# An attention and mixture-of-experts layer: routing work of VectorE gathered into fewer slots, and two PSUM readers moved behind the transposes

## The reference

```
xn  = layernorm(x)
att = attention(rmsnorm(xn) * norm_scale)      # 16 heads of 64, softmax over 512 keys, output projection + bias
lg  = silu(xn @ rw1 + rb1) @ rw2 + rb2         # router: 128 -> 512 -> 8 experts
top 2 of the 8 logits, softmax over the two    # the weights of a token
ffn = sum over its 2 experts of weight * (silu(xn @ w1[e] + b1[e]) @ w2[e] + b2[e])
out = x + att + ffn
```

## Time and profile before

| | |
|---|---|
| median of 3 runs | 2036.31 us (2034.46 to 2036.4) |
| profiled execution | 2034.46 us |
| its span, first to last instruction | 2032.5 us |
| TensorE busy | 1862.8 us, 92% |
| VectorE busy | 1629.2 us, 80% |
| ScalarE busy | 1238.5 us, 61% |
| GpSimd busy | 706.7 us, 35% |
| chain that ended last | TensorE 29%, VectorE 29%, ScalarE 27%, issue 13% |
| mean granted clock of TensorE | 0.994 |

### The profile page before, as it was taken

One profiled execution on the slowest core, in us unless ns is written; L12 is line 12 of the kernel. 1 busy time (PEld: TensorE's weight loads), 2 busy tenths in 40 slices (PEclk: granted clock), 3 DMA queues, 4 the chain that ended last, 5 costly groups with the idle time before them and its releaser, 6 DMA issues.

```text
span 2032.5 us, 72807 instructions
## 1 busy us (share of the span) xinstructions
PE 1862.8 (92%) x31718; PEld 1106.8 (54%) x31718; DVE 1629.2 (80%) x2274; ACT 1238.5 (61%) x3009; POOL 706.7 (35%) x624
## 2 busy tenths in 40 slices
PE   8898888889988888989899999999999999999996
PEld 5554455555545555555455555555555555555554
DVE  6887888888888888888988787878787777777774
ACT  5555556555665566556566666666757575757562
POOL 3243543344444333433102423333324132423142
PEclk9999999999999999999999999999999999999999
DMA  3033221111111111111323333433334334333342
GB/s 95 15 77 101 75 88 51 35 44 44 45 34 44 42 32 28 44 39 39 86 78 76 71 80 66 85 67 78 72 73 73 77 67 84 69 77 70 70 70 48
DMA packets 148863, 127.48 MB, mean 63 GB/s; under 512 B 27040, under 2 KB 133408, under 8 KB 148512
## 3 DMA queue, kind: packets, MB, share of 16 engines
q1 hardware_dynamic: 117952, 102.10, 18.8%
q0 software_dynamic: 30592, 20.73, 7.6%
HBM read 90.59 MB, written 34.27 MB: 61 GB/s over the span
## 4 chain that ended last, share of the span: by engine, by line
PE 29%; DVE 29%; ACT 27%; issue 13%; DMA 2%; SPq 0%; POOL 0%; POOLq 0%; DVEq 0%; ACTq 0%
ACT PR L907 19%; DVE NM L568 12%; DVE PT L576 7%; PE pair L469 7%; PE pair L330 6%; PE pair L311 6%; DVE OT L585 3%; ACT ZZ L996 3%; PE pair L343 2%; ACT ZT L993 2%; PE pair L272 2%; DVE HH L811 1%; PE pair L296 1%; PE pair L240 1%; PE pair L223 1%
## 5 line engine op out<-in xcount | busy, mean ns | idle before, releaser
L907 ACT ACTIVATE PR<-pair,NM 128x512 f32<-128x512 f32 x1024 | 690.5, 686 | 566.3 <-DVE NM L568 566.1
L576 DVE STREAM_TRANSPOSE PT<-PR 128x1024 f32<-128x1024 f32 x512 | 630.1, 1239 | 90.4 <-ACT PR L907 72.7
L568 DVE TENSOR_REDUCE NM<-pair 128x2 f32<-128x1024 f32 x512 | 599.8, 1212 | 52.6 <-PE pair L311 52.2
L311 PE MATMUL pair<-KS,QS 64*32 64x512 f32 x8192 | 505.7, 597 | 13.1 <-ACT KS L883 6.7
L330 PE MATMUL pair<-PT,V 32*64 32x256 f32 x16384 | 482.0, 378 | 15.8 <-issue 7.1
L1157 POOL DMA_INDIRECT out<-YS,IDW x156 | 245.1, 1571 | 657.8 <-DVE YS L818 612.1
L330 PEld LDWEIGHTS pair<-PT,V 32*64 32x64 f32 x16384 | 380.0, 131 | 167.6 <-issue 118.4
L311 PEld LDWEIGHTS pair<-KS,QS 64*32 64x32 f32 x8192 | 126.1, 106 | 242.4 <-issue 174.0
L811 DVE SCALAR_TENSOR_TENSOR HH<-ZT,ZZ 128x512 f32<-128x512 f32 x156 | 104.9, 692 | 171.6 <-ACT ZT L993 95.7
L1106 POOL TENSOR_TENSOR TH<-TH,HS 128x512 f32<-128x512 f32 x64 | 81.8, 1277 | 376.2 <-ACT HS L947 376.2
L907 ACT ACTIVATION_READ_ACCUMULATOR PR<-pair,NM 128x1 f32 x1024 | 208.0, 203 | 0.0
(11 more groups left out here) (130 smaller groups left out, 1743.1 us busy)
## 6 DMA issues: line engine op xcount, KB each, us to landing
RB<-l_rows SPq DMA_DIRECT2D x128, 256.0 KB
E<-w_tab SPq DMA_DIRECT2D x39, 512.0 KB
XG<-slots SPq DMA_DIRECT2D x39, 264.0 KB, 4.2
E<-in_w SPq DMA_DIRECT2D x39, 256.0 KB, 4.1
xin<-in_x SPq DMA_DIRECT2D x16, 256.0 KB
XQ<-in_x SPq DMA_DIRECT2D x16, 256.0 KB
l_rows<-RT SPq DMA_DIRECT2D x256, 2.0 KB
w_tab<-SPL SPq DMA_DIRECT2D x8, 512.0 KB, 2.7
```

The source lines that it names most:

```text
L311: m = pe.do.matmul(bank[2 * (s % 2) + r][32 * c:32 * c + 32, :], QS[rows, u % 2, c, at:at + 32], KS[rows, g % 2, c, :], start=True, stop=T ...
L568: dve.do.tensor_reduce(NM[:, step % 4], pairs[s % 2][:], AX.X, ALU.max, negate=True).then_inc(sem["dve_max"])
L576: dve.do.transpose(PT[:].rearrange("p c k q -> p (c k) q")[:, :, 32 * slot:32 * slot + 32], PR[:, step % PRB].rearrange("p r k -> p (r k)" ...
L907: act.do.activation(PR[:, step % PRB, r, :], bank[2 * (s % 2) + r], ACT.Exp, bias=NM[:, step % 4, r:r + 1], accum_out=RS[:, g % 2, r, at:a ...
```

## The change

On VectorE, `turn_logits` (L643) moves from h = 7 to the start of the next block's h = 0, ahead of `split_x`; `best` moves to the end of h = 0; `second`, `second_place` (now one function) and `counts` all stand at the end of h = 1; `place` stands in h = 2. `moments` and `variances` become one function, `stats`, in h = 3. `attending`, which holds `finish` and `full_h`, moves behind the two transposes, in every slot of the kernel.

On TensorE, `place` moves from the start of h = 3 to h = 2, behind the queries and ahead of the router; `turn_logits` moves within h = 7 from ahead of the keys and values to behind them. `totals` moves from slot 131 to slot 130. On GpSimd the scatter moves from h = 4 and 5 to h = 3 and 4, `power` from h = 6 to h = 4, and the first `attention_rows` from slot 7 to slot 5.

```diff
 # TensorE
             def route(G):
                 r, h = divmod(G, 8)
+                if 0 < r <= NB and h == 2:
+                    place(r - 1)
...
                 if h == 6:
                     logits(r)
+                if h == 7:
+                    turn_logits(r)
                 if r + 1 < NB and h == 7:
                     turn_x(r + 1)
-
-            def routing(G):
-                r, h = divmod(G, 8)
-                if 0 < r <= NB and h == 3:
-                    place(r - 1)
-                if r < NB and h == 7:
-                    turn_logits(r)
...
-                if G == EARLY * GB + 3:
+                if G == EARLY * GB + 2:
                     totals()
...
-                routing(G)
                 attending(G)
                 route(G)
 # VectorE
             def turned(G):
                 r, h = divmod(G, 8)
+                if h == 0 and 0 < r <= NB:
+                    turn_logits(r - 1)
                 if h == 0 and 0 < r < NB:
                     split_x(r)
...
                     if h == 0:
+                        best(r - 1)
+                    if h == 1:
                         second(r - 1)
-                    if h == 1:
-                        second_place(r - 1)
+                        counts(r - 1)
                     if h == 2:
-                        counts(r - 1)
-                    if h == 3:
                         place(r - 1)
-                if r < NB and h == 7:
-                    turn_logits(r)
-                    best(r)
-                if r + 1 < NB and h == 5:
-                    moments(r + 1)
-                if r + 1 < NB and h == 6:
-                    variances(r + 1)
+                if r + 1 < NB and h == 3:
+                    stats(r + 1)
...
-                attending(G)
                 for i, c in LATE[G]:
                     halves(i, c)
                 if u < UNITS:
                     turn_probs(u, 2 * k)
                     turn_probs(u, 2 * k + 1)
+                attending(G)
                 route(G)
 # GpSimd
-                if h == (1 if b else 7) and b + 1 < NB:
+                if h == (1 if b else 5) and b + 1 < NB:
                     attention_rows(b + 1)
...
-                if r == NB and h == 4:
+                if r == NB and h == 3:
                     scatter(r - 1, slice(0, 8), [0] * 8)
-                if 0 < r < NB and h in (4, 5):
-                    scatter(r - 1, slice(4 * h - 16, 4 * h - 12), [2 * G + 1, 2 * G + 1, 2 * G + 2, 2 * G + 2])
+                if 0 < r < NB and h in (3, 4):
+                    scatter(r - 1, slice(4 * h - 12, 4 * h - 8), [2 * G + 1, 2 * G + 1, 2 * G + 2, 2 * G + 2])
...
                 if r + 1 < NB:
+                    if h == 4:
+                        power(r + 1)
                     if h == 6:
-                        power(r + 1)
                         routed_rows(r + 1)
```

More of the change, by code:

```diff
@@ L524, in _, with stats @@
             dve = Engine(eng)
-            def moments(r):
+            def stats(r):
                 dve.wait_ge(*side("xq", r))
@@ L530, in moments @@
                     dve.do.bn_stats(bn[:, t, :], XQ[:, r % 2, t, :]).then_inc(sem["dve_bn"])
-            def variances(r):
                 dve.wait_ge(sem["dve_bn"], QT * r + QT)
@@ L684, in second @@
                 dve.do.scalar_tensor_tensor(flat(code), flat(eq), -64.0, iota72, ALU.mult, ALU.add).then_inc(sem["dve_gate"])
-            def second_place(r):
-                at = 15 * r
                 dve.wait_ge(sem["dve_gate"], at + 10)
@@ L838, in _ @@
             dve.do.memset(PR[:, 2, 1, :], 1.0).then_inc(sem["dve_ones"])
-            moments(0)
-            variances(0)
+            stats(0)
             first_rows()
```

## The result

The changed kernel takes 2058.86 us, the median of 4 runs (2052.96 to 2063.3), against 2036.21 us for the kernel before beside it: a ratio of 1.0111, with a 95% interval of 1.0086 to 1.0138. It is 22.6 us slower; 23 were forecast. Its profiled execution took 2063.62 us, some 5 us more than the median, so the two traces differ by 29.0 us of span and not by 22.6.

What follows compares the result with a forecast made beforehand. TensorE was taken to bound the expert stretch (96% busy), with routing (88%) paced by VectorE's path in slots 0 to 2. Terms: 22.2 - 22.5 - 5.0 + 13.7 + 12.6 + 2 = +23.0 us, so 2057 us, range 2044 to 2075.

Steps and rivals of the forecast that it cites:

- full_h: Moved behind the transposes: nothing, its bank being free before slot 2's projection wants it; at most 0.75 us, 15 times.
- (e): Routing slot 6, every second block: finish behind the transposes frees its bank late, mean 1.96 us, 7 times: +13.7 us.
- (f): Expert stretch: the turn of the expert's rows waits for finish's bank, mean 1.8 us, 7 times: +12.6 us.
- (a): Slots 7 to 0: logits turned behind keys and values; slot 0's maxima start earlier, gaining 1.35 us a block.
- (b): Routing slots 0 to 2: VectorE's bunched small work lengthens the path by 2.83 us; with (a), +22.2 us over 15 blocks.
- the clock: Slot 2: low-clock matmuls after TensorE's long wait, falling on the queries: +2 us, bounds 0 and 25.
- (c): Slot 3: the places leave it, removing TensorE work and a bank wait; 1.5 us, 15 times: -22.5 us.
- (d): Slot 6: VectorE's statistics no longer stand ahead of OT, which TensorE awaits; 0.62 us, 8 blocks: -5.0 us.
- The rule of the prediction: Slot 6: finish's bank comes free 5.24 plus 0.68 us after VectorE's maxima (NM) start.
- The rival that the bunched work is hidden: Slots 0 to 2: bunched work costs nothing and the bank waits come back whole; faster, 2020 us, chance 0.08.
- No change: TensorE does not meet the banks of finish, so (e) and (f) cost nothing: 2031 us, chance 0.06.
- Slower still: Slot 2: a low-clock spell falls on the projection in every block, 15 times 1.5 us more: 2080 us, chance 0.10.

Runs made afterwards that it cites:

- e3: The changed kernel with only finish put back ahead of the transposes, full_h staying behind them: 2018.99 us, 0.9927 of the kernel before.
- e2: The kernel before with only attending (finish and full_h) moved behind the transposes: 2074.49 us, 1.0199 of the kernel before.
- e1: The changed kernel with attending (finish and full_h) put back ahead of the transposes: 2028.8 us, 0.9978 of the kernel before.
- e4: The kernel before with six chained small VectorE ops added at the end of slot 1 in 15 blocks: 2065.13 us, 1.0155.
- e5: The kernel before with six chained small VectorE ops added at the end of slot 3 in 15 blocks: 2025.86 us, 0.9974.
- n1: The kernel before with only VectorE's two bank-freeing reads (L643, L718) moved ahead of the transposes: 1993.75 us, 0.9798.
- n2: n1 with moments in slot 3 instead of 5: 1981.37 us, 0.9744; on another chip 1981.61 us, 0.9728.
- f1: The kernel before with full_h alone moved behind the transposes, on a slower third chip: 2212.77 us, 1.001 of the kernel before.
- n3: n2 with full_h alone moved behind the transposes: 2171.25 us, 0.9823 on the third chip; 1983.49 us, 0.9744 on a fourth.

## Why the prediction was right

The forecast was +23.0 us, and +22.6 was measured. The mechanisms are those forecast: the bank waits go, the gathered work costs about what they gave, and `finish` behind the transposes makes the loss. That the sum agrees to half a microsecond is partly luck, for some sizes are off and cancel. `finish`, (e) and (f), was forecast at +26.3 us and measures +37.5 (after against e3, by the ratios). In the kernel before it measures +41.9 (e2), where its expectation said 38.6, since the statistics still stand ahead of OT there. All the rest was forecast at -3.3 us and measures -13.6 (e3 against before). Of this, 9.8 is the move of `full_h`; without it the rest is -3.8 (e1).

- **(a)** right: NM of slot 0 at T7 + 8.31, forecast 8.4.
- **(b)** right in kind. The work of VectorE behind the transposes of slots 0 and 1 makes the path longer by 0.67 and 1.54 us in the block shown (forecast 0.72 and 1.36). The router product and the projection behind the wait for QS add 2.27 us where 0.75 was forecast; the other 1.5 is the low clock. Seven of the 15 full blocks have 30.7 to 31.4 us from T7 to T3, as forecast; the other eight have 31.7 to 33.8. All 15 together take 26.3 us more, forecast 22.2 and 2 for the clock. The wait for QS ahead of a router product was to stand in every block and does so in six; in the others slow queries and router products fill most of it. e4 shows that VectorE in slot 1 is on the path, and e5 that in slot 3 it isn't.
- **(c)** right: T3 to T5 is 13.23 to 13.29 us in 11 of the blocks, forecast 13.3; -25.0 in all, forecast -22.5. That GpSimd's products beside `place` cost nothing was a hidden assumption: they cost 4.5 to 5 us in a block of e1 where `place` comes late.
- **(d)** too large: -5.0 forecast for the 8 blocks without `finish`; there T6 to T7 takes 3.7 us less in the kernel after, and 3.8 less from n1 to n2. (The -7.9 from n1 to n2 is over all 16 blocks; in those with `finish` the prediction counts this gain inside (e).)
- **(e)** right to the hundredth in what frees the bank, wrong in what follows. (Its own working gives +2.12 where it writes +2.16, which is 0.1 us in all.) The rule of the prediction, NM + 5.24 + 0.68, gives 539.48 in the block shown, and the projection starts at 539.49. It then takes 3.49 us instead of 1.93. The seven blocks with `finish` take 77.15 us from T6 to T7, where the rule gives 69.9 (56.14 before, and 7 x 1.96); the difference of 7.3 is the low clock on the projection. The wait itself is 2.77 us, longer than the 1.2 to 1.9 that I had named to look for; I had given there what T7 loses, and not what TensorE waits, which begins earlier since NM comes 0.75 us sooner.
- **(f)** right for the wait. In the expert stretch TensorE waits for `finish` 13.6 us, 7 times (forecast 12.6); from e3 to after slots 144 to 255 grow by 18.3 us. Against the trace before, three of the seven blocks lose 1.6 to 1.9 us from slot 6 to slot 7, as forecast; the other four lose 2.4 to 3.8 us. Three of these four have a spell of the low clock (3.4 to 3.8 us).

TensorE in two calls of `finish` in the expert stretch of the kernel after, the first with the earlier trace rows:

```profile
1132.10 0.63 PE L240 MATMUL pair<-idn,XG 128*128 128x128 f32 x4 [1.78 <-DVE xin L614]
...
1406.13 1.09 PE L240 MATMUL pair<-idn,XG 128*128 128x128 f32 x4 [2.38 <-DVE xin L614]
```

NM stands at 1126.08, so the first turn begins at NM + 6.02, forecast NM + 5.97. In the second the four matmuls of the same turn take 1.09 us instead of 0.63: a spell again.

- **`full_h`** "nothing": right in the kernel before (f1) and in n2, wrong in the changed kernel, where its move keeps `place` clear of GpSimd (-9.8 us). What the prediction left out is that ahead of the transposes VectorE can wait for a late turn (1.76 us in e1), and what that does to the ops behind.
- **The clock** is the term that was mis-sized: 2 us forecast, with bounds of 0 and 25. Read off as the part of (b), (e) and (f) that exceeds their working, it is about 4 + 7 + 5 = 16 us. The whole of TensorE's slow work is more, since some of it fills waits: busy time in slots 0 to 130 grew by 29.7 us. That the 16 us are the clock's is argued from durations. No run takes all spells away and leaves the waits, but the pair of calls in e2 does it for one wait (1.5 us). I had placed the spell on the queries, where it is mostly covered, and there it fell in 14 of 16 blocks. All seven blocks at 30.7 to 31.4 us have it there. What I had left out is the spells that last longer or come behind the *next* wait and so reach the projection (32.2 to 33.7 us in three blocks), and those behind `finish`. The rule cited in the prediction (the Trainium skill, "TensorE: Matmul & The Clock Gate", section "HAM oscillation — how this bites in real kernels"), that the array falls back again and again, was the better guide; the trace agrees, with a spell in slot 2 of each of 16 blocks.

The rival that the bunched work is hidden is refuted by OT in slot 2 (T2 + 4.28) and by e4. "No change" is refuted by e2. "Slower still" was partly true: the low clock was on the projection of slot 2 in 4 of 16 blocks, not in all.

## What to carry to other kernels

When products take banks in turn, moving one reader moves its wait to whoever takes that bank next. Move the single read that frees the bank, and leave the chain behind it: n1 did that in the gap of the exponentials for 38 us, while the change moved whole chains and lost 23. Where engines alternate, ask of each place whether a microsecond there is paid: 1.3 us were free in slot 3 and cost 2.2 in slot 1. And compare waits and busy time over the same work: here the waits of the routing half shrank by 15 us while it grew longer by 14.5.

## What was not expected of the hardware

- A wait of 2 to 4 us of TensorE can be paid twice, since the matmuls behind it may run at the lower clock. Behind the waits of 2.9 to 4.0 us for OT a spell came 16 times of 16 in the kernel after. Behind the waits of 2.0 to 2.8 us for `finish` in the routing stretch it came 7 times of 7 there and 3 of 7 in e2; the projection then took up to 3.66 us instead of 1.99.
- VectorE's small multiplies, adds and casts take about 1 us instead of 0.1 to 0.2 beside a product of GpSimd (1.27 us). Where several such ops form a chain, each can lose up to a whole product of GpSimd: together 3.8 us for the four of `place` in e1, 2.9 for the four adds of `counts` in e4.
- TensorE can fall behind with no semaphore wait that the profile shows: once for 4.66 us in the kernel before, and on one chip in slot 5 of every block but the first, some 10 us each, in part at the lower clock. It goes there with GpSimd's scatter in that slot; no run settles the cause. n3's ratio is 0.982 there and 0.974 on another chip.
